# Transposed attention probabilities of two heads in four: by VectorE and DRAM instead of TensorE

## The reference, cut to what matters

```python
q = (x @ wq).reshape(b, t, 16, 128); k, v = (x @ wk), (x @ wv)   # 4 heads each, repeated 4 times
scores = q @ k.T / sqrt(128)            # masked above the diagonal, softmax in float32
out = softmax(scores) @ v
x = layernorm(x + out @ wo)
logits = clip(x @ gate_w.T, -50, 50)    # top 2 of 8 experts, softmax over the two
x = layernorm(x + x @ W.T + sum of the chosen experts' sparse deltas applied to x)
```

## Time and profile before

| | us |
|---|---|
| median of 3 runs | 1836.31 |
| lowest and highest | 1833.64, 1836.33 |
| the profiled execution, its own time | 1836.27 |
| its span, first to last instruction | 1834.5 |
| mean granted TensorE clock | 0.991 of full speed |

### The profile page before, as it was taken

The page is one execution under the profiler, slowest core; times in us unless marked ns, Lnnn a source line. Parts: engine busy times, 40 slices in busy tenths (PEclk is TensorE's granted clock), DMA queues, the critical chain, the costliest instruction groups (busy, mean ns, idle before and its releaser), DMA issues.

```text
span 1834.5 us, 33331 instructions
## 1 busy us (share of the span) xinstructions
PE 1774.3 (97%) x9290; PEld 1502.0 (82%) x9290; DVE 1238.0 (67%) x3881; ACT 823.1 (45%) x2058; POOL 799.0 (44%) x1093
## 2 busy tenths in 40 slices
PE   8999999999999999999999999999999999999982
PEld 7888888888888888888888888888888888778872
DVE  5566467776777577757775777677776777763355
ACT  4444344434444444544454444454444443434454
POOL 6775345544554333323332333233323334666564
PEclk9999999999999999999999999999999999999996
DMA  9665443335333455454444445454445338545788
GB/s 329 223 226 195 164 141 116 116 110 168 116 116 110 150 162 153 150 174 149 154 150 159 134 152 160 154 177 158 150 133 198 135 107 314 173 161 166 251 314 318
DMA packets 156287, 315.83 MB, mean 172 GB/s; under 512 B 23008, under 2 KB 66176, under 8 KB 145600
## 3 DMA queue, kind: packets, MB, share of 16 engines
q1 hardware_dynamic: 137808, 273.74, 44.2%
q0 software_dynamic: 18288, 39.80, 7.1%
HBM read 226.25 MB, written 87.23 MB: 171 GB/s over the span
## 4 chain that ended last, share of the span: by engine, by line
PE 85%; DVE 4%; issue 3%; POOL 2%; DMA 2%; ACT 1%; DVEq 0%; POOLq 0%; ACTq 0%; SPq 0%
PE psum L1541 23%; PE psum L1543 23%; PE psum L1542 23%; PE psum L1568 7%; PE psum L2298 2%; PE psum L2299 2%; PE psum L2300 2%; PE psum L372 1%; DMA token_rows<-x,ids_now 1%; ACT probs L1818 1%; PE psum L788 1%; DVE pT_lo L1942 1%; POOL expert_weights L1435 1%; POOL probs L1415 0%; DMA chosen_rows<-y_rows,slot_now 0%
## 5 line engine op out<-in xcount | busy, mean ns | idle before, releaser
L1415 POOL TENSOR_SCALAR probs<-probs,row_inv 128x128 f32<-128x128 f32 (+3 forms) x512 | 308.0, 625 | 435.1 <-DVE row_inv L1939 433.2
L1818 ACT ACTIVATE probs<-probs,neg_max 128x512 f32<-128x512 f32 (+3 forms) x512 | 282.4, 554 | 361.4 <-DVE neg_max L1931 359.4
L1541 PE MATMUL psum<-xT_hi,w_hi 128*128 128x512 f32 x640 | 252.5, 394 | 0.7 <-DVE qT_lo L1956 0.7
L1931 DVE CUSTOM_DVE_ANT_0 probs<-psum,causal 128x512 f32<-128x512 f32 (+3 forms) x512 | 223.4, 487 | 42.7 <-issue 20.4
L1543 PE MATMUL psum<-xT_hi,w_lo 128*128 128x512 f32 x640 | 250.2, 391 | 0.0
L1542 PE MATMUL psum<-xT_lo,w_hi 128*128 128x512 f32 x640 | 249.9, 390 | 0.0
L1942 DVE TENSOR_TENSOR pT_lo<-psum,pT_hi 128x512 fp32r<-128x512 f32 (+1 forms) x384 | 206.5, 593 | 19.7 <-ACT pT_hi L1828 19.5
L1828 ACT CAST pT_hi<-psum 128x512 fp32r<-128x512 f32 (+1 forms) x384 | 172.3, 526 | 65.2 <-PE psum L1568 65.2
L1541 PE MATMUL psum<-wo_hi,oT_hi 128*128 128x512 f32 x496 | 196.8, 397 | 0.0
L1543 PE MATMUL psum<-wo_hi,oT_lo 128*128 128x512 f32 x496 | 194.0, 391 | 0.0
L1542 PE MATMUL psum<-wo_lo,oT_hi 128*128 128x512 f32 x496 | 193.6, 390 | 0.0
(11 more groups left out here) (250 smaller groups left out, 3870.4 us busy)
## 6 DMA issues: line engine op xcount, KB each, us to landing
w_hi<-split_qk_weights SPq DMA_DIRECT2D x140, 256.0 KB, 2.7
w_lo<-split_qk_weights SPq DMA_DIRECT2D x140, 256.0 KB, 3.0
wo_hi<-split_out_weights SPq DMA_DIRECT2D x27, 1024.0 KB, 5.5
wo_lo<-split_out_weights SPq DMA_DIRECT2D x27, 1024.0 KB, 7.6
expert_weights_hi_lo<-split_expert_weights SPq DMA_DIRECT2D x8, 2048.0 KB, 10.0
x_in<-in_L_attn_x_dram SPq DMA_DIRECT2D x8, 1024.0 KB, 7.3
expert_weights<-fill SPq DMA_DIRECT2D x16, 512.0 KB, 4.4
piece_raw<-expert_weights SPq DMA_DIRECT2D x16, 512.0 KB, 5.9
```

The source lines that it names most:

```text
L1415: last = pool.tensor_scalar(p, p, row_inv[:, buf, i:i + 1], 1.0, ALU.mult, ALU.mult)
L1541: pe.matmul(dst, hi_s, hi_m, start=start, stop=False)
L1818: last = act.activation(probs[:, buf, a:a + w], probs[:, buf, a:a + w], ACT.Exp, bias=neg_max[:, buf, i:i + 1], scale=-1.0, accum_out=row_ ...
L1931: last = dve.tensor_tensor_reduce(probs[:, buf, a:a + w], psum[:, BANK_S + bank, col:col + w], causal[:, T - w:T], -1.0, -MASKED, ALU.add, ...
```

## The change

It concerns the 27 groups of batches 1 to 7 except the last group ("moved" groups: route set and kind not "end"). In these, heads n and n+2 are no longer turned by TensorE:
- VectorE turns each 32x32 square of the normalized rows in place (`turn_blocks`, five instructions, 1280 elements per partition);
- SyncE stores the result to DRAM (640 KB), waits, and loads it back with four DMAs of 160 KB so that the squares land in the right partitions (`move`);
- ScalarE copies it in one instruction to pT hi and VectorE subtracts in one instruction for pT lo (`moved_pT`), both reading SBUF.

The order around it changes as the diff shows. TensorE in a moved "group": scores(n+1), query(n+2), filler(1), scores(n+2), filler(2), transposes(n+1), query(n+3), filler(3), scores(n+3), key, values_first, query(n+4), query(n+5), transposes(n+3), scores(n+4), values_second, and as before. In a moved "batch" group key stays behind values_first, and the turning of x of the next batch moves (chunks 0, 1 behind filler(3), chunks 2, 3 behind scores(n+3)). In a moved "first" group: scores(n+1), query(n+2), value row 0, scores(n+2), value row 1, transposes(n+1), query(n+3), value row 2, scores(n+3), value row 3, key, values_first. The piece buffers go from two to one.

On SyncE, and where it is called: first in the queue of the group, and behind the weights of the last query:

```diff
+        def move(it, k, free):
+
+
+            wait_apart(sp, s_blocks, moved_number(it, k) + 1, s_passed)
+            sp.dma_start(strips[k], F.blocks[:].rearrange("p j f -> p (j f)")).then_inc(s_moved, 16)
+            wait_apart(sp, s_pt_lo, free, s_passed)
+            wait_apart(sp, s_moved, 32 + MOVES * moved_number(it, k), s_passed)
+            for j in range(SIDE):
+                src = strips[k, :, j * PACK // SIDE:(j + 1) * PACK // SIDE].rearrange("(i p) f -> p i f", p=SQUARE)
+                sp.dma_start(F.moved[j * SQUARE:(j + 1) * SQUARE], src).then_inc(s_moved, 16)
+
...
+            if is_moved(kind, route):
+                move(it, 0, 3 * n)
...
             slot(4, it + 1, after)
...
+            if is_moved(kind, route):
+                move(it, 1, 3 * (n + 2) + 3)
```

On GpSimd the routing's rstd goes behind a normalize, and in a first group behind normalize(n+2):

```diff
-            if route and kind != "first":
+            if route and kind == "end":
                 route_rstd(pool, R, it - TT)
             normalize(n + 1, 1)
+            if route and kind not in ("first", "end"):
+                route_rstd(pool, R, it - TT)
```

On TensorE:

```diff
             scores(n + 1, 1)
+            if moved:
+                pe.wait_ge(s_q_lo, n + 2)
+                query(2, it, BANK_A)
...
             filler(0 if kind == "first" else 1)
-            pe.wait_ge(s_q_lo, n + 2)
-            if not route and kind == "first":
-                pe.wait_ge(N.s_wT, C)
-            query(2, it, BANK_A)
+            if moved:
+                scores(n + 2, 0)
...
+            key_first = kind == "first" or moved and kind == "group"
+            if key_first:
                 pe.wait_ge(s_q_lo, n + 4)
                 key(it + 1)
             values_first()
-            if kind in ("group", "batch"):
+            if not key_first:
                 pe.wait_ge(s_q_lo, n + 4)
```

On ScalarE (the second call of `moved_pT` stands behind qT(n+5) and ahead of `route_exp` and pT(n+3); the first behind qT(n+3) and ahead of exps(n+3)):

```diff
+        def moved_pT(n, it, k):
+
+            act.wait_ge(s_moved, 16 + MOVES * (moved_number(it, k) + 1))
+            act.wait_ge(s_o, n + 2 * k)
+            act.copy(pT_hi[:, 0].rearrange("p (b i c) -> p b i c", i=SIDE, c=SQUARE),
+                     F.moved[:].rearrange("p i (b c) -> p b i c", c=SQUARE)).then_inc(s_pt_hi, 3)
```

On VectorE:

```diff
+        def turn_blocks(n, it, k):
+
+
+            dve.wait_ge(s_norm, n + 2 * k + 1)
+            dve.wait_ge(s_moved, 16 + MOVES * moved_number(it, k))
+            blocks = F.blocks[:].rearrange("p j (b c) -> p b j c", c=SQUARE)
+            for i in range(TT):
+                keys = range(min(i + 1, TT - 1))
+                at = [KEY_AT[j] // P + i - j for j in keys]
+                src = probs[:, 0, ROW_AT[i]:ROW_AT[i] + len(keys) * P].rearrange("p (b j c) -> p b j c", j=SIDE, c=SQUARE)
+                last = dve.transpose(blocks[:, at[0]:at[-1] + 1:3], src)
+            j, at = TT - 1, KEY_AT[TT - 1] // P
+            src = probs[:, 0, ROW_AT[j] + j * P:ROW_AT[j] + T].rearrange("p (b j c) -> p b j c", j=SIDE, c=SQUARE)
+            dve.transpose(blocks[:, at:at + 1], src).then_inc(s_blocks, 1)
+
+        def moved_pT(n, k):
+
+            dve.wait_ge(s_pt_hi, 3 * (n + 2 * k) + (6 if k == 0 else 3))
+            view = "p (b i c) -> p b i c"
+            low(pT_lo[:, 0].rearrange(view, i=SIDE, c=SQUARE), pT_hi[:, 0].rearrange(view, i=SIDE, c=SQUARE),
+                F.moved[:].rearrange("p i (b c) -> p b i c", c=SQUARE), s_pt_lo, 3)
...
             maxima(n + 1, 1)
+            if moved:
+                turn_blocks(n, it, 0)
+                inverse(n + 1, 1)
+                qT(n + 2, 0, BANK_A)
...
             if kind != "first":
                 add_rows(it - 1, 1, "group")
-            inverse(n + 1, 1)
+            if moved:
+                maxima(n + 2, 0)
...
                 qT(n + 3, 1, BANK_A)
+            if moved:
+                turn_blocks(n, it, 1)
+            if early and moved:
+                route_logits(dve, R, tt, (2,), products)
+            if moved:
+                moved_pT(n, 0)
...
                 qT(n + 5, 1, bank_of_query(1, kind))
-                pT(n + 3, 1)
+                if moved:
+                    moved_pT(n, 1)
+                pT(n, 3, moved)
                 maxima(n + 4, 0)
```

More of the change, by code:

```diff
@@ L1723, in iteration @@
                 pe.wait_ge(N.s_read, g)
-            transposes(n, 0)
+            if not moved:
+                transposes(n, 0, kind, route)
             if kind == "end":
@@ L1729, in iteration @@
                 filler(1 if kind == "first" else 2)
-            transposes(n + 1, 1)
-            scores(n + 2, 0)
+            transposes(n, 1, kind, route)
+            if not moved:
+                scores(n + 2, 0)
             if kind == "end":
@@ L1734, in iteration @@
                 return
-            if kind == "first":
+            if kind == "first" and not moved:
                 filler(2)
@@ L1738, in iteration @@
             query(3, it, BANK_A)
-            if kind == "batch":
-                turn_x(b + 1, (0, 1))
+            if kind == "first" and moved:
+                filler(2)
+                scores(n + 3, 1)
+            if kind == "batch" and not moved:
+                turn_x(b + 1, (0, 1), route)
             filler(3)
             if kind == "batch":
-                turn_x(b + 1, (2, 3))
-            scores(n + 3, 1)
-            if kind == "first":
+                turn_x(b + 1, (0, 1) if moved else (2, 3), route)
+            if not (kind == "first" and moved):
+                scores(n + 3, 1)
+            if kind == "batch" and moved:
+                turn_x(b + 1, (2, 3), route)
+            key_first = kind == "first" or moved and kind == "group"
+            if key_first:
                 pe.wait_ge(s_q_lo, n + 4)
@@ L1878, in iteration @@
                 qT(n + 3, 1, BANK_A)
-            pT(n + 1, 1)
-            exps(n + 2, 0)
-            if kind == "first":
+            pT(it, 1, kind, route)
+            if not moved:
+                exps(n + 2, 0)
+            if kind == "first" and not moved:
                 v(b, 2)
@@ L1885, in iteration @@
             if kind == "first":
+                v(b, 2 if moved else 3)
+            if moved:
+                moved_pT(n, it, 0)
+            if kind == "batch":
+                high_xT(act, F, psum, b + 1, range(C // 2) if moved else range(C), BANKS_PT[:2])
+            exps(n + 3, 1)
+            if kind == "first" and moved:
                 v(b, 3)
-            if kind == "batch":
-                high_xT(act, F, psum, b + 1, range(C), BANKS_PT[:2])
-            exps(n + 3, 1)
-            if kind == "first":
+            if kind == "batch" and moved:
+                high_xT(act, F, psum, b + 1, range(C // 2, C), BANKS_PT[:2])
+            key_first = kind == "first" or moved and kind == "group"
+            if key_first:
                 kT(it + 1)
@@ L1898, in iteration @@
                 oT(n, 0, kind)
-                if kind in ("group", "batch"):
+                if not key_first:
                     kT(it + 1)
-                pT(n + 2, 0)
+                if not moved:
+                    pT(it, 2, kind, route)
             if kind != "end":
@@ L2037, in iteration @@
                 route_normalize(dve, R, tt)
-            inverse(n + 2, 0)
-            if early:
+            if not moved:
+                inverse(n + 2, 0)
+            if early and not moved:
                 route_logits(dve, R, tt, (2, 3), products)
@@ L2053, in iteration @@
             if kind == "batch":
+                low_xT(dve, F, psum, b + 1, (0, 1) if moved else (2, 3), BANKS_PT[:2])
+            maxima(n + 3, 1)
+            if early and moved:
+                route_logits(dve, R, tt, (3,), products)
+            if kind == "batch" and moved:
                 low_xT(dve, F, psum, b + 1, (2, 3), BANKS_PT[:2])
-            maxima(n + 3, 1)
             if route:
@@ L2068, in iteration @@
             if kind == "end":
-                pT(n + 2, 0)
+                pT(n, 2, moved)
             if route:
@@ L2082, in iteration @@
                 count_later(dve, N, upper, q)
-            if kind in ("group", "batch"):
+            if not key_first and kind != "end":
                 kT(it + 1)
-            if kind != "end":
-                pT(n + 2, 0)
+            if kind != "end" and not moved:
+                pT(n, 2, moved)
             if route:
```

170 lines of the change are left out of this document (107 added, 63 removed).

## The result

The changed kernel takes 1948.71 us (median of 4 runs, 1942.55 to 1950.06) against 1835.54 (4 runs, one more than in the table above, 1833.64 to 1836.33): 1.0612 times, 95% interval 1.0587 to 1.0636. The prediction was 1951, 1912 to 2010. The sign, the three waits and the size came true. Two terms of the sum were wrong by about 25 us each, in opposite directions.

What follows compares the result with a forecast made beforehand. TensorE, busy for 97% of the span, was taken as the bound, if operands come in time. 14 x 3.05 ("group") + 6 x 4.5 ("batch") + 7 x 6.5 ("first") = 115 us more: 1951 us, range 1912 to 2010.

Steps and rivals of the forecast that it cites:

- Removed: Ten transposes a head leave TensorE in 54 heads, with a bank wait in 20 groups: 63 us together.
- Wait A: TensorE at scores(n+2) waits 1.68 us for the third query's lo; about 2.0 in a "first" group.
- Wait B: At values_second, head n+2's copy and subtraction stand ahead of the pT splits: 2.1 us lost in each of 27 groups.
- Wait C: In 14 "group" groups query(n+4) waits for the bank of pair 0's second half: 1.65 us.
- Prices: Per head: five VectorE transposes 1.75 us, subtraction 1.40, ScalarE copy 1.40; store of 640 KB 4.1, loads about 3.
- Rivals 2: Unknown VectorE prices near their upper end (transposes 3.5 us, or subtraction 2.8): 2018 us; chance 17%.
- rival 3: Prices at the lower bounds (transposes 0.9, copy 1.1): 89 us added together, 1925 us; chance 15%.
- 4: Strips late for head n, so ScalarE waits in front of exps(n+3): 1980 to 2000 us; chance 12%.
- The "first" group: Seven moved groups, +6.5 us each, from late maxima, routing rows and value row 3.
- value row 3: In a "first" group its split ends at t 33.4, TensorE is there at t 30.6: 2.9 us of wait.
- The clock: Waits of 2 to 3 us could bring the granted clock down, putting the time above the range; no term in the sum.

Runs made afterwards that it cites:

- t: Changed kernel with four of the five VectorE transposes left out in 40 of the 54 heads; 1932.69 us, 1.0548 times the kernel before.
- a: Changed kernel with qT(n+2) made ahead of exps(n+1) on ScalarE and ahead of turn_blocks on VectorE; 1954.65 us, 1.0661 times the kernel before.
- b: Changed kernel with head n+2's copy ahead of the second query's hi (ScalarE), its subtraction ahead of that query's lo (VectorE); 1886.78 us, 1.0283.
- c: Changed kernel with the PSUM bank order of a "first" group used in the 14 moved "group" groups; 1938.38 us, 1.0576 times the kernel before.
- abcdfvx: Changed kernel with the edits of ad, b, c and bfv, and head n+2 of a "batch" turned behind maxima(n+3); 1800.75 us, 0.9829 times the kernel before.
- ad: Changed kernel with the edit of a, and output row 1 added ahead of the routing's variance on VectorE; 1950.96 us, 1.066 times the kernel before.
- bfv: Changed kernel with the edit of b; in "first" groups, routing load ahead of head n's strips, value row 3 ahead of scores(n+3) and exps(n+3); 1857.13 us, 1.0126.

## Why the prediction was right, and where its sum was wrong

**Removed, right.** The work fell by 47.6 us although TensorE has 85 waits more. With 0.16 us of restart behind each, 13.6 us together, some 61 were removed, an estimate; predicted 63.

**Wait A, right, with its mechanism.** Predicted 1.68, measured 1.69 (start to start 1.91 instead of 0.22; idle 1.52, and 1.78 in the six "batch" groups). VectorE's and ScalarE's timelines of the same group: maxima at t 4.81, exps' last read at t 7.65, hi at t 7.74, lo from t 8.35 to 9.04 (predicted 9.02):

```profile
955.77 0.69 DVE L2020 CUSTOM_DVE_ANT_0 probs<-psum,causal 128x512 f32<-128x512 f32 x1
...
958.90 0.27 DVE L2046 STREAM_TRANSPOSE probs_blocks<-probs 128x128 f32<-128x128 f32 x1
...
959.31 0.69 DVE L2068 SCALAR_TENSOR_TENSOR qT_lo<-psum,qT_hi 128x512 fp32r<-128x512 f32 x1
```

```profile
958.70 0.57 ACT L1904 ACTIVATE qT_hi<-psum 128x512 fp32r<-128x512 f32 x1
```

Experiment t shows that free transposes don't shorten it; a shows what was behind it, the addition of output row 1, so that the wait alone was worth next to nothing. The prediction's 0.15 for semaphore and restart stands in no row of it; from the end of lo to the matmul it was 0.13 here.

**Wait B and C, right.** Wait B: 1.96 idle, 2.1 with its restart (predicted 2.1), in 27 groups. Wait C: 1.45 idle, 1.6 with its restart (1.65), in 12 of the 14 groups; in the two of the last batch it is 2.8 idle, and 1.4 there in t. b and c show the causes by taking each away.

**Prices, right or on the dear side.** Groups by shape after, VectorE and ScalarE:

```profile
L2031 DVE TENSOR_TENSOR pT_lo<-probs_moved,pT_hi 128x1280 fp32r<-128x1280 f32 x54 | 80.4, 1488 | 15.2 <-ACT pT_hi L1892 14.4 <-DVE route_logits L700 0.4
...
L2043 DVE STREAM_TRANSPOSE probs_blocks<-probs 128x384 f32<-128x384 f32 x108 | 53.7, 536 | 0.0
...
L2043 DVE STREAM_TRANSPOSE probs_blocks<-probs 128x256 f32<-128x256 f32 x54 | 21.7, 402 | 0.0
...
L2043 DVE STREAM_TRANSPOSE probs_blocks<-probs 128x128 f32<-128x128 f32 x54 | 16.4, 304 | 0.0
```

```profile
L1892 ACT CAST pT_hi<-probs_moved 128x1280 fp32r<-128x1280 f32 x54 | 67.9, 1257 | 0.0
```

Five transposes take 1.67 us to the next instruction (957.42 to 959.09; predicted 1.75): these transposes cost VectorE about what a dense copy of their size costs (536 ns for 384 elements; 549 by the prediction's 1.04 an element and 0.15). The subtraction took 1.49, 1.41 to the next instruction (predicted 1.40), the copy 1.26 (predicted 1.40), the store of 640 KB 2.9 (4.1), the loads 3.3 (3). Rivals 2 and 3, which lived on prices far from these, are out, and so is 4: no DMA is among ScalarE's waits for the strips.

**The "first" group, wrong.** Predicted +6.5, measured +4.6, of which 1.5 is the clock's, so about +3. The step that failed is the time at which VectorE comes to the last part of maxima(n+1). I took t 7.0 from the earlier trace rows, where it stands behind 2.27 us of "issue"; in this group after, the whole is read at t 5.2:

```profile
854.57 0.09 DVE L2020 DVE_READ_ACCUMULATOR2_ANT neg_max<- 128x1 f32 x1
```

Such a gap in front of the last part, 2.2 to 2.4 us, stands in four of the seven "first" groups before, but in only one after. In that one (it starts at 429.49, so t 7.08) wait A is there as predicted, 2.29 against about 2.0:

```profile
436.57 0.42 DVE L2020 CUSTOM_DVE_ANT_0 probs<-psum,causal 128x256 f32<-128x256 f32 x1 [2.19 <-issue]
```

```profile
439.43 0.49 PE L1587 MATMUL psum<-kT_hi,qT_hi 128*128 128x512 f32 x1 [2.29 <-DVE qT_lo L2068]
```

What makes the gap was not found. Without it the blocks left 2.3 us sooner (t 6.9 and not 9.2). With the cheaper store the routing rows came in time; the prediction's own terms for them, 9.2 + 4.1 + 1.5 + 3.4, also make 18.2 and not 19. TensorE's timeline of that group has, in the place of 2.0 and 1.7, waits of 0.23 and 0.34, and for value row 3 2.62 (predicted 2.9):

```profile
857.29 0.49 PE L1587 MATMUL psum<-kT_hi,qT_hi 128*128 128x512 f32 x1 [0.23 <-DVE qT_lo L2068]
...
869.11 0.49 PE L1587 MATMUL psum<-kT_hi,qT_hi 128*128 128x512 f32 x1 [0.34 <-DVE qT_lo L2068]
...
879.38 0.49 PE L1587 MATMUL psum<-pT_hi,v_hi 128*128 128x512 f32 x1 [2.62 <-POOL v_lo L1443]
```

Seven groups by 3.4 to 3.5 are some 24 us too much. One row with an idle time put down to "issue" is no place to read an order of work from before the other groups have been looked at.

**The clock, left out of the sum.** The prediction named it as something that would put the time above its range. It cost 26 us (42.8 against 16.5) and only filled what the "first" groups had left. With the measured sizes and no clock the sum is 14 x 3.14 + 6 x 4.1 + 7 x 3.1 = 90 us, and with the clock 116 against 113 measured. So 1951 for 1949 is in part luck; the range held either way. The 90 us are rival 3's 89 by chance, since the prices were not its.

**"Slower" was the order's verdict, not that of the turning.** Turning two heads in four on VectorE does save TensorE 61 us. What lost them was where the edits left the copies, the bank and the loads; with the seven edits of abcdfvx the same turning is 1.7% faster than the kernel before.

## What to carry to other kernels

When work is taken off the engine that bounds, write down for each operand of its next steps when it is ready and when it is now wanted; each step that comes sooner than its operand turns saving into wait, and a wait undone alone may only show the next one. Price the clock with the waits: the account span = work + waits + clock told ten kernels apart here, and an edit that shortens waits can be paid back by the clock. Put a copy that is wanted late behind one that is wanted soon only after asking whose chain ends last, and keep small loads with near readers ahead of large transfers in a queue.

## What the runs showed that was not expected

In all ten kernels with moved heads, each stretch of slow matmuls that lasted over two or more of them between 200 and 1800 us began at or within 3.1 us behind a wait of TensorE of 1.78 us or more (14 after, 20 in a, 29 in ad, none in abcdfvx). Behind shorter waits there was none: bfv has 27 of 1.2 to 1.6 us and 6 of 1.78, and its only stretch of slow matmuls stands behind 2.76. Nor did each long wait bring one. One behind a wait B costs 1.5 us (20 matmuls take 5.5 to 5.6 us instead of 4.05). Of 27 equal waits of 1.96 us, 6 were followed by one in t, 10 in the changed kernel, 12 in a, 16 in c and 19 in ad, so an edit elsewhere moved this by 10 us and more; why was not found.
